# Tile 0 projected from x loaded turned, with its mean taken off by products with 1/512, and two quarters of Wq used ahead of K/V

## What is computed

```python
h = layernorm(x)                            # no weights, eps 1e-5
q = rope(h @ Wq)                            # 32 heads of 16
k, v = rope(ctx @ Wk), ctx @ Wv             # 8 heads of 16, each used by 4 heads of q
x = x + softmax(q @ k.T / 4) @ v @ Wo
h = layernorm(x)
gate = softmax over the top 16 of (h @ Wq_w.T @ keys.T), 64 experts, 0 elsewhere
x = x + 2 * ((h @ A_w.T) * gate, each expert's weight on its 8 columns) @ B_w.T
```

## Time and profile before

| | us |
|---|---|
| median of three runs | 166.45 |
| lowest, highest | 166.23, 168.49 |
| the profiled execution | 166.19 |
| its span, from the first to the last instruction | 163.6 |
| TensorE busy in the span | 158.4 |

### The profile page before, as it was taken

The page is one execution under the profiler, slowest core; times in us unless marked ns, Lnnn a source line. Parts: engine busy times, 40 slices in busy tenths (PEclk is TensorE's granted clock), DMA queues, the critical chain, the costliest instruction groups (busy, mean ns, idle before and its releaser), DMA issues.

```text
span 163.6 us, 4199 instructions
## 1 busy us (share of the span) xinstructions
PE 158.4 (97%) x1437; PEld 128.7 (79%) x1437; DVE 135.8 (83%) x394; ACT 95.5 (58%) x215; POOL 89.6 (55%) x115
## 2 busy tenths in 40 slices
PE   6799999999999999999999999999999999999993
PEld 2557886777889787979787987979799986789883
DVE  1979896997998999799888998799886997868562
ACT  3598999899675463933678238832478064414210
POOL 6389999999969944625932098106360305220300
PEclk9999999999999999999999999999999999999999
DMA  5999961403312283434623342133410001000013
GB/s 162 356 411 393 409 221 68 134 31 98 92 48 50 79 251 97 116 112 100 166 85 94 81 105 56 50 98 87 107 62 23 4 0 55 11 6 0 0 64 128
DMA packets 12116, 18.45 MB, mean 113 GB/s; under 512 B 2496, under 2 KB 5056, under 8 KB 11840
## 3 DMA queue, kind: packets, MB, share of 16 engines
q1 hardware_dynamic: 10944, 16.36, 31.7%
q10 hardware_dynamic: 1152, 1.84, 3.7%
HBM read 11.11 MB, written 2.10 MB: 81 GB/s over the span
## 4 chain that ended last, share of the span: by engine, by line
PE 95%; DVE 2%; issue 1%; ACT 0%
PE ps_w L1365 14%; PE ps_w L1370 13%; PE ps_w L1366 12%; PE ps_t L1378 8%; PE ps_w L1358 4%; PE ps_s L1451 4%; PE ps_w L1360 3%; PE ps_w L1359 3%; PE ps_s L1470 3%; PE ps_s L1521 3%; PE ps_t L1521 3%; PE ps_s L1491 2%; PE ps_s L1504 2%; PE ps_t L1370 2%; PE ps_t L1366 2%; PE ps_t L1365 2%
## 5 line engine op out<-in xcount | busy, mean ns | idle before, releaser
L476 POOL TENSOR_TENSOR late<-late,gate 128x512 f32<-128x512 f32 x7 | 7.6, 1087 | 34.3 <-DVE gate L1147 19.3
L707 ACT ACTIVATE eT<-ps_s 128x512 f32<-128x512 f32 x32 | 17.1, 602 | 1.7 <-PE ps_s L1491 0.9
L461 POOL TENSOR_TENSOR oT_lo<-o_n,oT_hi 128x512 fp32r<-128x512 f32 x8 | 10.4, 1296 | 5.3 <-ACT oT_hi L715 5.3
L1365 PE MATMUL ps_w<-am_hi,x2T_hi 128*128 128x288 f32 x44 | 12.6, 308 | 0.0
L1366 PE MATMUL ps_w<-am_lo,x2T_hi 128*128 128x288 f32 x44 | 12.0, 295 | 0.0
L1365 PE MATMUL ps_w<-b_hi,zT_hi 128*128 128x512 f32 (+1 forms) x28 | 11.1, 402 | 0.0
L759 ACT ACTIVATE zT_hi<-ps_t 128x512 fp32r<-128x512 f32 x7 | 4.2, 598 | 11.7 <-PE ps_t L1378 11.7
L1358 PE MATMUL ps_w<-wq_hi,xT_hi 128*128 128x512 f32 x26 | 10.9, 418 | 0.0
L1038 DVE TENSOR_REDUCE ps_s<-ps_s 128x8 f32<-128x512 f32 x16 | 10.6, 688 | 0.3 <-PE ps_s L1451 0.2
L1048 DVE TENSOR_REDUCE ps_s<-ps_s 128x8 f32<-128x512 f32 x16 | 10.4, 691 | 0.5 <-PE ps_s L1470 0.3
L406 POOL TENSOR_TENSOR rstd<-ve,neg_half 128x1 f32<-128x1 f32 x8 | 4.4, 554 | 11.5 <-DVE ve L966 10.2
(11 more groups left out here) (283 smaller groups left out, 551.7 us busy)
## 6 DMA issues: line engine op xcount, KB each, us to landing
x_sb<-x SPq DMA_DIRECT2D x8, 256.0 KB, 6.4
...
cT_in<-cT SPq DMA_DIRECT2D x6, 256.0 KB, 4.1
wq_sb<-wq SPq DMA_DIRECT2D x4, 256.0 KB, 4.4
...
```

Of the source, the lines that this page charges most:

```text
L461: pool.tensor_tensor(oT_lo[:], o_n[:].rearrange("p (b r q) -> p r b q", b=2, r=REP), oT_hi[:].bitcast(F32), ALU.subtract).then_inc(oT_lo_o ...
L707: act.activation(eT[:, c].rearrange("p b n -> p (b n)"), ps_s[:, c, :], ACT.Exp)\
L1365: pe.matmul(dst, hi(k), w_hi[:, k, cols], start=(k == 0), stop=False)
```

## The change

- The first load is tile 0 of `xT`, straight into `xT_raw`. Quarters 0 and 1 of Wq follow it, ahead of context and Wkv; quarters 2 and 3 come behind Wkv, each with an ordinary x tile (0 and 1, still needed for statistics and for the residual) in front of it.
- TensorE multiplies a 128x128 matrix of 1/512 (`share`, in the first 128 columns of `xh`) with the four chunks of the turned x. This leaves in every row of `ps_t0` the mean of each token. VectorE subtracts it from `xT_raw` in place. The four turns of `xh` for tile 0 and ScalarE's copy go.
- The deviation of tile 0 is no longer applied to x but to the rotary table (`cs_0`), which VectorE scales by `rstd0` before it rotates Q; the statistics of tile 0 move behind the angles, and those of tile 1 ahead of `rotate_k(0)`.
- TensorE does Q over quarters 0 and 1, then all of K/V of tile 0, then Q over quarters 2 and 3.
- GpSimd makes `pick` first, starts its low parts when the mean has been taken off, with Wq's first two in front, and makes all four of Wkv's; VectorE makes `sel` at the start and no low part of Wkv. ScalarE takes the high parts in the new order of arrival, and its table load for Exp ahead of `values_out(0)`.

```diff
@@ -239,7 +241,8 @@
...
-        ld_xT = {t: sem(f"ld_xT{t}") for t in range(DIRECT, T)}
+        ld_xT = {t: sem(f"ld_xT{t}") for t in (0, *range(DIRECT, T))}
+        share_ok, cs_0_ok = sem("share_ok"), sem("cs_0_ok")
@@ -344,14 +347,16 @@
...
-            load_x(0)
+            sp.dma_start(xT_raw[:], xT[0]).then_inc(ld_xT[0], 16)
+            for k in range(2):
+                sp.dma_start(wq_sb[:, k, :], wq[k]).then_inc(ld_wq[k], 16)
...
-            for k in range(DK):
+            for k in range(2, DK):
+                load_x(k - 2)
...
-            load_x(1)
@@ -399,11 +404,11 @@
...
-                if t >= 1:
-                    pool.wait_ge(xh_ok, min(t, DIRECT))
+                if t >= 2:
+                    pool.wait_ge(xh_ok, min(t, DIRECT) - 1)
...
-                pool.tensor_tensor(rstd1[:], ve1[:], neg_half[:], ALU.pow).then_inc(rstd1_ok, 1)
+                pool.tensor_tensor((rstd1 if t else rstd0)[:], ve1[:], neg_half[:], ALU.pow).then_inc(rstd1_ok, 1)
@@ -494,30 +504,27 @@
...
-            pool.memset(pick[:], 0.0).then_inc(pick_ok, 1)
...
-            pool.wait_ge(pick_ok, 1)
-            pool.affine_select(out=pick[:], in_=pick[:], compare_op=ALU.not_equal, fill=1.0, base=0,
-                               pattern=[[-(QUAD + 2), PAIRS], [-2 * KVH, 2], [-KVH, 2], [-1, 2]],
-                               channel_multiplier=1).then_inc(pick_ok, 1)
...
+                pool.wait_ge(x_raw_ok, 1)
+                for k in range(2):
+                    split_lo(wq_lo, wq_sb, wq_hi, wq_h, wq_l, k)
...
-                pool.wait_ge(rope_step, 9)
-                for k in range(2):
-                    split_lo(wkv_lo, wkv_sb, wkv_hi, wkv_h, wkv_l, k)
-                split_lo(wq_lo, wq_sb, wq_hi, wq_h, wq_l, 0)
-                split_lo(wkv_lo, wkv_sb, wkv_hi, wkv_h, wkv_l, 2)
+                split_lo(wkv_lo, wkv_sb, wkv_hi, wkv_h, wkv_l, 0)
...
-                split_lo(wq_lo, wq_sb, wq_hi, wq_h, wq_l, 1)
+                split_lo(wkv_lo, wkv_sb, wkv_hi, wkv_h, wkv_l, 1)
...
-                split_lo(wq_lo, wq_sb, wq_hi, wq_h, wq_l, 2)
-                split_lo(wq_lo, wq_sb, wq_hi, wq_h, wq_l, 3)
+                for k in range(2, DK):
+                    split_lo(wq_lo, wq_sb, wq_hi, wq_h, wq_l, k)
+                split_lo(wkv_lo, wkv_sb, wkv_hi, wkv_h, wkv_l, 2)
...
+                split_lo(wkv_lo, wkv_sb, wkv_hi, wkv_h, wkv_l, 3)
@@ -759,39 +766,34 @@
...
-            def x_raw(t):
-                act.wait_ge(xhT_ps, t + 1)
-                if t >= 1:
-                    act.wait_ge(q_ps, t)
-                act.activation(xT_raw[:], xhT_bank(t)[:].rearrange("p (k q) -> p k q", k=DK), ACT.Copy)\
-                   .then_inc(x_raw_ok, 1)
...
-                for k in range(DK):
-                    act.wait_ge(ld_wkv[k // 2], 16)
+                for k in range(2):
+                    act.wait_ge(ld_wq[k], 16)
+                    split_hi(wq_hi, wq_sb, wq_h, k)
+                for k in range(2):
+                    act.wait_ge(ld_wkv[0], 16)
...
-                x_raw(0)
...
-                for k in range(2):
-                    act.wait_ge(ld_wq[k], 16)
-                    split_hi(wq_hi, wq_sb, wq_h, k)
+                for k in range(2, DK):
+                    act.wait_ge(ld_wkv[1], 16)
+                    split_hi(wkv_hi, wkv_sb, wkv_h, k)
+                act.wait_ge(ld_wq[2], 16)
+                split_hi(wq_hi, wq_sb, wq_h, 2)
+                act.activation(preload[:, 1:2], half_pi[:], ACT.Exp)
...
-                act.activation(preload[:, 1:2], half_pi[:], ACT.Exp)
...
-                act.wait_ge(ld_wq[2], 16)
-                split_hi(wq_hi, wq_sb, wq_h, 2)
+                act.wait_ge(ld_wq[3], 16)
+                split_hi(wq_hi, wq_sb, wq_h, 3)
...
-                act.wait_ge(ld_wq[3], 16)
-                split_hi(wq_hi, wq_sb, wq_h, 3)
@@ -956,11 +958,10 @@
...
+                if t >= 1:
+                    dve.wait_ge(rstd1_ok, t)
...
-                    dve.wait_ge(rstd1_ok, t)
-                else:
-                    dve.wait_ge(xh_ok, 1)
@@ -973,6 +974,9 @@
...
+            def table_0(at, n):
+                return cs_0[:, at:at + HD].rearrange("p (s j) -> p s j", s=2).unsqueeze(1).broadcast_to([P, n, 2, J])
@@ -1188,12 +1192,12 @@
...
-                dve.wait_ge(ld_x[0], 16)
-                dve.bn_stats(bn1[:], x_sb[:, 0, :]).then_inc(stat1, 1)
-                dve.wait_ge(stat1, 1)
-                dve.bn_aggr(mv1[:], bn1[:]).then_inc(stat1, 1)
-                dve.wait_ge(stat1, 2)
-                dve.tensor_scalar_add(ve1[:], mv1[:, 1:2], EPS).then_inc(stat1, 1)
+                dve.memset(share, 1.0 / D).then_inc(share_ok, 1)
+                dve.wait_ge(pick_ok, 2)
+                dve.reduce_sum(pick_sum[:], pick[:].rearrange("p c j b h -> p b h c j"), AX.XY).then_inc(sel_ok, 1)
+                dve.wait_ge(sel_ok, 1)
+                dve.tensor_copy(sel[:].rearrange("p b (h k) -> p b h k", h=2),
+                                pick_sum[:].unsqueeze(3).broadcast_to([P, 2, 2, BATCH])).then_inc(sel_ok, 1)
@@ -1203,13 +1207,14 @@
...
+                dve.wait_ge(xhT_ps, 1)
+                dve.tensor_tensor(xT_raw[:], xT_raw[:],
+                                  xhT_bank(0)[:, 0:P].unsqueeze(1).broadcast_to([P, DK, P]), ALU.subtract)\
+                   .then_inc(x_raw_ok, 1)
...
-                dve.wait_ge(rstd1_ok, 1)
-                dve.tensor_scalar(xh[:], x_sb[:, 0, :], mv1[:, 0:1], rstd1[:], ALU.subtract, ALU.mult)\
-                   .then_inc(xh_ok, 1)
@@ -1221,23 +1226,21 @@
...
-                dve.wait_ge(pick_ok, 2)
-                dve.reduce_sum(pick_sum[:], pick[:].rearrange("p c j b h -> p b h c j"), AX.XY).then_inc(sel_ok, 1)
-                dve.wait_ge(sel_ok, 1)
-                dve.tensor_copy(sel[:].rearrange("p b (h k) -> p b h k", h=2),
-                                pick_sum[:].unsqueeze(3).broadcast_to([P, 2, 2, BATCH])).then_inc(sel_ok, 1)
-                split_lo(wkv_lo, wkv_sb, wkv_hi, wkv_h, wkv_l_late, 3)
+                statistics1(0)
+                statistics1(1)
+                H = REP * KVH
+                w = ps_w0[:].rearrange("p (h s j) -> p h s j", h=H, s=2)
...
-                statistics1(1)
+                dve.wait_ge(rstd1_ok, 1)
+                dve.tensor_scalar(cs_0[:], cs[:, 0, :], rstd0[:], None, ALU.mult).then_inc(cs_0_ok, 1)
...
-                H = REP * KVH
-                w = ps_w0[:].rearrange("p (h s j) -> p h s j", h=H, s=2)
+                dve.wait_ge(cs_0_ok, 1)
...
-                                  table(HD, 0, H), ALU.mult).then_inc(q_rot, 1)
+                                  table_0(HD, H), ALU.mult).then_inc(q_rot, 1)
...
-                dve.tensor_tensor(w, w, table(0, 0, H), ALU.mult).then_inc(q_rot, 1)
+                dve.tensor_tensor(w, w, table_0(0, H), ALU.mult).then_inc(q_rot, 1)
@@ -1432,7 +1434,8 @@
...
-                pe.wait_ge(kT_lo_ok, t + 1)
+                if t >= 1:
+                    pe.wait_ge(kT_lo_ok, t + 1)
@@ -1584,22 +1587,29 @@
...
-                pe.wait_ge(x_raw_ok, t + 1)
+                pe.wait_ge(x_raw_ok, 1)
...
-                pe.wait_ge(ident_ok, 1)
+                pe.wait_ge(share_ok, 1)
+                pe.wait_ge(ld_xT[0], 16)
+                for k in range(DK):
+                    mm = pe.matmul(xhT_bank(0)[:, 0:P], share, xT_raw[:, k, :], start=(k == 0), stop=(k == DK - 1))
+                mm.then_inc(xhT_ps, 1)
+                for k in range(2):
+                    pe.wait_ge(ld_wq[k], 16)
+                    raw_q(0, k)
...
-                turn_xh(0)
...
-                for k in range(DK):
+                for k in range(2, DK):
...
+                pe.wait_ge(ident_ok, 1)
```

16 lines of the change are left out of this document (11 added, 5 removed).

## The result

| | before | after |
|---|---|---|
| median of six runs each, us | 166.6 | 168.11 |
| lowest, highest | 166.23, 168.49 | 167.37, 168.66 |
| the profiled execution | 166.19 | 168.28 |
| its span | 163.6 | 166.4 |

The changed kernel is slower, by a ratio of 1.0106 with an interval of 1.0075 to 1.0138. That is inside the 2% that was called no change, but it is 1.5 us where 0.45 was forecast, and the median lies above the range of 165.7 to 167.9. The direction was right and the size was wrong by a factor of three.

The account below looks back on a forecast made before the run. TensorE, busy 158.4 of 163.6 us, was taken as the bound. K/V of tile 1 starting 0.45 us later goes through to the end: 166.64 from the profiled execution, 166.90 from the median; forecast 166.8, range 165.7 to 167.9.

Parts of the forecast that it names:

- Step 1: TensorE's own work: four turns (0.44) go, mean products (0.9, bounds 0.44 and 1.10) come; net 0.46 us more.
- Step 2: TensorE's start: mean products at 4.69, subtraction 0.69, Q at 6.38; a 0.79 us wait replaces 0.92, 0.13 won.
- Step 3: TensorE from Q at 6.38: K/V of tile 1 at 12.04 by its own work, 0.34 us later; loads don't stop it.
- Step 4: ScalarE's late value copy, behind VectorE's K rotation, holds K/V of tile 1 until about 12.15: 0.45 us later than 11.70.
- Step 5: VectorE after Q: scaling the tables gives q_r at about 14.3, just hidden; 0.1 to 0.4 if GpSimd slows it.
- Step 6: GpSimd's stage-one list, with a fourth Wkv rest, ends 0.9 us later; margins 0.65 and 0.78 hold, cost 0.
- rival B: GpSimd becomes the bound between 20 and 45 us and holds TensorE: 0.3 to 1.0 more, 167.1 to 167.8; chance 0.15.
- Rival A: The new start is a small gain, from cheaper mean products, subtraction and earlier x: 165.5 to 166.2 us; chance 0.22.
- Rival C: TensorE's clock falls to 1.2 GHz in the middle of Q: 169.8 to 172.4 us; chance 0.05.

Follow-up runs that it names:

- experiment 5: The changed kernel with the six angle steps ahead of the subtraction and seven or five warm-up products in place of nine: 167.22 us (seven), 166.73 us (five).
- experiment 1: The changed kernel with the six angle steps moved ahead of the subtraction on VectorE: 166.45 us, ratio 1.0018 against the kernel before.
- experiment 7: The changed kernel with the six angle steps ahead of the subtraction and the mean products done twice: 167.7 us, ratio 1.0085 against the kernel before.
- experiment 4: The kernel before, with GpSimd's first low part no longer waiting for the last angle step: 166.31 us, ratio 1.0004.
- experiment 8: The changed kernel with early angle steps, Wkv loaded before Wq, K/V of tile 0 before Q: 168.66 us (six warm-up products), 168.32 us (nine).
- experiment 9: experiment 8 with GpSimd's low parts of Wq 0 and 1 forward: 167.55, 167.92 us; then also ScalarE's high part of quarter 1 forward: 166.42, 166.49 us.
- experiment 6: The changed kernel with early angle steps, five warm-up products, and tile 1's statistics behind K's rotation and the table scaling: 167.12 us, ratio 1.0085.

## Why the prediction was wrong

Of the 2.79 us at K/V of tile 1, 0.45 was forecast. Between 12.16 and 12.66 (experiments 5 and 1) lie 0.5 us: the warm-up ended 0.57 later than read and the mean products took 0.13 more than taken, both because the clock rose at 5.40 and not at 3.97. Between 12.66 and the changed kernel's 14.49 lie 1.83 us for the angle steps beside GpSimd and what they delay (some 1.6 of them, as the mean products differ by 0.22 between the two executions). Point by point:

- **Step 1**, mean products at 0.9: right for the full clock (the passes of the second set in experiment 7 make 0.90). They took 1.25 in the changed kernel's trace and 0.88 to 1.62 in the other kernels with nine warm-up products, since part of them ran before the clock had risen. The bounds of 0.44 and 1.10 left that out.
- **Step 2**, the mean products start at 4.69, Q at 6.38: they started at 5.26 and Q at 7.37. The nine warm-up products took 4.02 us and not 3.45. That was wrong in kind: 4.69 was read from one execution and taken as fixed, and in that execution the clock had risen at 3.97, earlier than in any other trace here. Before, it did not matter, since TensorE waited 0.92 us for Wkv behind it; the change removed this cover and put the warm-up's end on the path. The subtraction was right: 0.69, one wait of 0.87 ended by it (0.79 forecast).
- **Step 3**, 5.66 us from Q to K/V of tile 1 by TensorE's own work: 5.51 in experiment 1. Right. The loads did not stop it there.
- **Step 4**, the value copy holds K/V of tile 1 at 12.15: where neither failure acts (experiment 5), K/V starts at 12.16. The copy ended at 12.01 and the turn of K at 12.10, so the two are nearly even, as the forecast's 12.11 and 12.04 were. But "ScalarE's table load for Exp costs nothing: it is over near 11.6" failed: it started at 12.69, for ScalarE stood 2.9 us waiting for the last angle step.
- **Step 5 is the step that failed.** It lists VectorE's work behind Q and weighs contention with GpSimd for the scaling of the table (0.1 to 0.4), and step 2 excludes it for the subtraction. No step has the six angle steps, which the diff does not move in VectorE's text. What moved was GpSimd's wait, from behind them to ahead of them. The row that would have priced it was in my hand: the 256-column pass of 0.95 beside GpSimd in the earlier trace rows, of which the forecast says "seems to have slowed". It runs 0.42 alone (experiment 4), and what it waited for was the end of GpSimd's instruction. Read as a block, not as a slowdown, it gives each of the two steps of 0.22 that start beside a low part of 1.25 the price of that low part, 2.0 us more for both.
- **Step 6** and **rival B**: GpSimd's `cT_lo` of tile 2 was forecast 0.9 later by its own work. In experiment 1 it came at 19.79 against 18.57, 1.22 later with TensorE 0.96 later, and nothing waited. In the changed kernel it came 2.94 later, with TensorE 2.79 later. The margins held, so B did not happen in the change. Its mechanism is real, and cheaper to wake than I thought: in experiments 8 and 9 low parts out of place made TensorE wait 0.7 to 1.7 us, and in experiment 6 late statistics made it wait 0.8.
- **Rival A** (a gain) is out: no version had K/V of tile 1 earlier by 0.2 except one, and that one paid it back. **Rival C** by its sign did not happen: once risen, at 5.87, the granted clock stays 1.00, and Q's first half takes 1.96, its full-pace time with a fill. TensorE did not fall back behind a wait of 0.87, so the rule of the Trainium skill that is quoted there as a danger cost nothing in the change. In experiment 8 the clock did fall behind a wait of 1.72, at a price of 1.7 us. What the forecast's rivals lacked was the other end: a clock that rises later than in the one trace. The 1.000 read for the whole span does not cover the first 4 us, in which six of the nine products ran 0.43 apart.

What is shown is the cost of the meeting, of the late start and of the order of the low parts. Not settled is why the clock rises when it does: at 3.97 and 4.21 us in two traces of the old order, at 4.27 to 7.10 in fourteen of the new ones. One trace of each kernel can't tell whether the new order has a part in that. Not settled either is why the medians differ by 1.5 us and the profiled spans by 2.8, beyond the 0.8 us by which the span before was a low one.
